# Token weights of the experts: spread by a product on TensorE, or by broadcast reads from DRAM

## What is computed

```python
x = x + cross_attention(layernorm(x), ctx, ctx, mask, Wq, Wk, Wv, Wo)   # 16 heads of 8
flat = layernorm(x)                                                     # 2048 tokens x 128
logits = flat @ router_w.T                                              # 16 experts
topk_scores, topk_idx = top_k(logits + router_bias, 2)
combine[token, topk_idx] += softmax(topk_scores)                        # 2048 x 16, two entries per token
hidden = silu(gate_all(flat)) * up_all(flat)                            # each expert: 64 hidden features
out = sum over experts of combine * (hidden @ down) + shared_expert(flat)   # shared: 128 hidden features
x = x + out
```

## Time and profile before

| | us |
|---|---|
| device time, median of 3 runs | 201.56 (201.18 to 201.57) |
| span of the profiled execution | 199.7 |
| TensorE busy | 184.6 (92%) |
| VectorE busy | 169.6 (85%) |
| ScalarE busy | 128.1 (64%) |
| GpSimd busy | 94.5 (47%) |

### The profile page before, as it was taken

One profiled execution on the slowest core, in us unless ns is written; L12 is line 12 of the kernel. 1 busy time (PEld: TensorE's weight loads), 2 busy tenths in 40 slices (PEclk: granted clock), 3 DMA queues, 4 the chain that ended last, 5 costly groups with the idle time before them and its releaser, 6 DMA issues.

```text
span 199.7 us, 4422 instructions
## 1 busy us (share of the span) xinstructions
PE 184.6 (92%) x1389; PEld 132.0 (66%) x1397; DVE 169.6 (85%) x520; ACT 128.1 (64%) x298; POOL 94.5 (47%) x156
## 2 busy tenths in 40 slices
PE   7497599999999999999995999999999999999973
PEld 7375456566666666676683677677777777777742
DVE  6899999799899999999998789867887798778881
ACT  2195448789999889989986555564554544555531
POOL 6855992968888888888785802400000000000000
PEclk9999999999999999999999699999999999999999
DMA  5978700000000000000000000000100010001001
GB/s 130 302 219 207 303 14 0 5 0 3 2 3 2 0 0 0 0 3 0 5 2 0 0 3 0 0 0 0 54 3 0 0 53 0 0 0 53 0 0 53
DMA packets 8095, 7.07 MB, mean 35 GB/s; under 512 B 784, under 2 KB 7056, under 8 KB 7952
## 3 DMA queue, kind: packets, MB, share of 16 engines
q1 hardware_dynamic: 7504, 6.34, 10.4%
q10 hardware_dynamic: 576, 0.55, 1.1%
HBM read 5.84 MB, written 1.05 MB: 34 GB/s over the span
## 4 chain that ended last, share of the span: by engine, by line
PE 78%; DVE 7%; issue 1%; ACT 1%; DVEq 0%; ACTq 0%
PE bank L1026 38%; PE bank L982 14%; PE bank L964 7%; PE bank L973 5%; PE bank L1066 3%; PE bank L953 2%; PE bank L943 2%; DVE xn L678 2%; PE bank L933 2%; PE bank L938 1%; PE bank L922 1%; PE bank L949 1%; DVE v_all L805 1%; PE bank L1031 1%; PE bank L1038 1%
## 5 line engine op out<-in xcount | busy, mean ns | idle before, releaser
L613 ACT ACTIVATE sig<-bank 128x512 f32<-128x512 f32 x36 | 21.4, 598 | 34.9 <-PE bank L1026 34.6
L982 PE MATMUL bank<-k_blk,q_blk 128*128 128x512 f32 x64 | 34.0, 615 | 0.2 <-issue 0.2
L827 DVE TENSOR_TENSOR hid_u<-sig,bank 128x512 f32<-128x512 f32 x32 | 22.0, 686 | 13.3 <-PE bank L1026 10.2
L442 POOL TENSOR_TENSOR k_blk<-k_all,consts_sb 128x512 f32<-128x512 f32 x32 | 32.7, 1042 | 0.0
L1026 PE MATMUL bank<-xt_hi,w_hi 128*128 (+1 forms) x72 | 30.0, 416 | 0.0
L1026 PE MATMUL bank<-xt_hi,w_lo 128*128 (+1 forms) x72 | 28.8, 400 | 0.0
L1026 PE MATMUL bank<-xt_lo,w_hi 128*128 (+1 forms) x72 | 28.8, 400 | 0.0
L764 DVE TENSOR_REDUCE smax<-bank 128x8 f32<-128x512 f32 x32 | 22.0, 686 | 1.8 <-PE bank L982 1.8
L568 ACT COPY prob_t<-bank 128x512 f32<-128x512 f32 x32 | 18.7, 585 | 7.0 <-PE bank L964 6.7
L785 DVE TENSOR_TENSOR prob<-bank,smax 128x512 f32<-128x512 f32 x32 | 22.0, 687 | 0.6
L1026 PE MATMUL bank<-hid_hi,w_hi 128*128 128x512 f32 (+1 forms) x37 | 20.5, 554 | 1.1 <-DVE hid_lo L836 1.1
(11 more groups left out here) (127 smaller groups left out, 399.0 us busy)
## 6 DMA issues: line engine op xcount, KB each, us to landing
w_moe_sb<-w_moe SPq DMA_DIRECT2D x1, 1728.0 KB, 8.1
x_sb<-x SPq DMA_DIRECT2D x4, 256.0 KB, 7.4
ctxt_sb<-ctx_t SPq DMA_DIRECT2D x4, 256.0 KB, 6.1
ctx_sb<-ctx_nat SPq DMA_DIRECT2D x4, 256.0 KB, 5.1
out<-x_sb SPq DMA_DIRECT2D x3, 256.0 KB, 2.3
w_att_sb<-w_att ACTq DMA_DIRECT2D x1, 264.0 KB, 5.8
mrow<-mask_row ACTq DMA_DIRECT2D x1, 256.0 KB, 5.4
sel_sb<-expert_sel SPq DMA_DIRECT2D x1, 256.0 KB, 8.3
```

Of the source, the lines that this page charges most:

```text
L442: last = nc.gpsimd.tensor_tensor(k_blk[p][:, g, :, :], k_all[:, bass.ds(t, 1), g, :].broadcast_to([P, HG, S]), hmask_sb.rearrange("p (h o) ...
L613: nc.scalar.activation(sig[r][:, :], gate_ps[r][:, :], ACT.Silu).then_inc(s_sig, 1)
L827: nc.vector.tensor_tensor(dst[:, :], sig[r][:, :], up_ps[r][:, :], ALU.mult).then_inc(s_hid_u, 1)
L982: nc.tensor.matmul(score_ps[g][:, :], q_blk[q][:, g, :, :].rearrange("p b s -> p (b s)"), k_blk[q][:, g, :, :].rearrange("p h s -> p (h s) ...
```

## The change

`sel_sb`, `identb_sb`, `comb3` and the product `token_weights` go. `weights_as_rows` turns `comb` of a half (8 tiles x 16 experts on 128 columns) by one f32 transpose into a part of bank 2; it waits for the sum and for an earlier copy out of that bank, and `attention_transposed(15)`, which writes the same bank, now waits until the transpose is copied. `weights_to_sbuf` copies 128x128 elements into `comb_t`, for the first half between `silu(0,1)` and step 16. SP stores this to `w_rows` in DRAM, waits until it has landed, and then issues for each unit two broadcast loads: the row of one expert, 512 tokens, over 64 partitions, twice. The target `spread` is a ring of four buffers (`SPREADS`, in the memory of `mix_all`); a later round waits for `weighted` four units earlier. SP's `store_result` now stands between these loads. `weighted` waits for both loads and reads `spread`. `up` no longer waits for the bank of the spread weights. VectorE's routing of the first half ends with the sum. `half_tiles`, `two_weights` and `join_experts` are the old lines in functions of their own.

```diff
+        spread = [mix_all[:, k * GT:(k + 1) * GT, :].rearrange("p t k -> p (t k)") for k in range(SPREADS)]
+        w_rows = nc.dram_tensor("w_rows", [2, EXPERTS, TILES // 2, P], F32).ap()
...
-        def expert_weights(eng, ops, half, written):
...
-            for part in range(PARTS - 1):
-                ops.tensor_copy(comb3[:, :, part, :], comb[:, tiles, :]).then_inc(written, 1)
-                eng.wait_ge(written, 3 + 2 * part)
-                ops.tensor_tensor(comb[:, tiles, :], comb[:, tiles, :], comb3[:, :, part, :],
-                                  ALU.subtract).then_inc(written, 1)
-                eng.wait_ge(written, 4 + 2 * part)
-            ops.tensor_copy(comb3[:, :, PARTS - 1, :], comb[:, tiles, :]).then_inc(s_comb3, 1)
+        def weigh_experts(ops, half):
+            tiles = half_tiles(half)
             for k, dst in ((0, comb), (1, comb_b)):
+                last = ops.tensor_tensor(dst[:, tiles, :], dst[:, tiles, :],
+                                         w_top[:, tiles, k:k + 1].broadcast_to([P, TILES // 2, EXPERTS]), ALU.mult)
+            last.then_inc(s_route[half], 1)
+        def join_experts(eng, ops, half):
+            tiles = half_tiles(half)
+            eng.wait_ge(s_route[half], 1)
+            ops.tensor_tensor(comb[:, tiles, :], comb[:, tiles, :], comb_b[:, tiles, :], ALU.add).then_inc(s_comb[half], 1)
...
-            sp.dma_start(sel_sb[:, :, :], expert_sel).then_inc(s_wmoe, 16)
-            sp.dma_start(identb_sb[:, :], ident_bf).then_inc(s_wmoe, 16)
+            def store_rows(half):
+                sp.wait_ge(s_ct_sb, half + 1)
+                sp.dma_start(w_rows[half].rearrange("e t k -> t e k"), comb_t[half][:, :]).then_inc(s_w_rows, 16)
+            def spread_weights(n):
+                g, pair = divmod(n, EPAIRS)
+                if n >= SPREADS:
+                    sp.wait_ge(s_hid, n - SPREADS + 1)
+                for e in range(2):
+                    rows = w_rows[g // 2, 2 * pair + e, (g % 2) * GT:(g % 2 + 1) * GT, :]
+                    sp.dma_start(spread[n % SPREADS][e * E_DIM:(e + 1) * E_DIM, :],
+                                 rows.rearrange("(o t) k -> o (t k)", o=1).broadcast_to([E_DIM, GN]))\
+                        .then_inc(s_spread[n % SPREADS], 16)
...
+            store_rows(0)
+            sp.wait_ge(s_w_rows, 16)
+            for n in range(GROUPS * EPAIRS):
+                if n == EPAIRS + SPREADS:
+                    store_rows(1)
+                    sp.wait_ge(s_w_rows, 32)
+                spread_weights(n)
+                if n >= EPAIRS and n % EPAIRS == SPREADS + 1:
+                    store_result(n // EPAIRS - 1)
+            for n in range(GROUPS - 1, GROUPS + 1):
+                store_result(n)
...
-            nc.gpsimd.memset(comb_t[:, :].bitcast(F32), 0.0).then_inc(s_comb_zero, 1)
...
+            def weights_to_sbuf(half):
+                act.wait_ge(s_ct, half + 1)
+                nc.scalar.copy(comb_t[half][:, :], ct_ps[half]).then_inc(s_ct_sb, 1)
...
             silu(0, 1)
+            weights_to_sbuf(0)
             peel(step, TILES)
-            weights_to_sbuf(0, cb_ps[0], slice(0, GN))
             high_part(0, 1)
-            weights_to_sbuf(1, cb_ps[0], slice(GN, 2 * GN))
...
             def weighted(g, m):
                 dve.wait_ge(s_hid_u, n + 1)
-                dve.wait_ge(s_cb, g * EPAIRS + m)
-                nc.vector.tensor_tensor(hid[m % 3][:, :], hid_u[r][:, :], cb_ps[r][:, :], ALU.mult).then_inc(s_hid, 1)
+                k, turns = (m - 1) % SPREADS, EPAIRS // SPREADS
+                dve.wait_ge(s_spread[k], (g * turns + (m - 1) // SPREADS + 1) * 32)
+                nc.vector.tensor_tensor(hid[m % 3][:, :], hid_u[r][:, :], spread[k], ALU.mult).then_inc(s_hid, 1)
...
+            def weights_as_rows(half):
+                pe.wait_ge(s_comb[half], 1)
+                pe.wait_ge(s_at_sb, TILES - 1 + half)
+                nc.tensor.transpose(ct_ps[half], comb[:, half_tiles(half), :].rearrange("p t e -> p (t e)"),
+                                    ident_sb).then_inc(s_ct, 1)
...
-            def token_weights(g, m):
-                pe.wait_ge(s_ct_sb, min(m, 2) if isinstance(g, int) else 4)
-                nc.tensor.matmul(cb_ps[m % 2][:, :], sel_sb[:, m - 1, :], comb_t[:, bass.ds(g * GN, GN)], start=True,
-                                 stop=True).then_inc(s_cb, 1)
...
             up(0, 1)
+            weights_as_rows(0)
+            pe.wait_ge(s_ct_sb, 1)
             attention_transposed(TILES - 1, 1)
-            weights_as_rows(0, cb_ps[0])
```

## The result

The changed kernel takes 196.66 us (median of 4 runs, 195.19 to 197.24) where the kernel before takes 201.56 (201.18 to 201.88): a ratio of 0.9743, 95% interval 0.9701 to 0.9786. The time lies in the range of the prediction (192.2 to 197.0), but above its forecast of 192.4 to 194.4, 3.3 us over the 193.4 that it named. The profiled execution is the slowest of the four (197.24, span 195.4), so the traces miss by a little more than the medians: 195.4 against the 191.5 us that the sum gave for the span.

A forecast was written before the change was run, and what follows sets the result against it. TensorE, never idle in the expert stage, was taken as the bound. Hand-over 1.4 + products 6.7 + transposes 0.4 - VectorE's other work 0.3 = 8.2 us, so 201.56 falls to 193.4 us (forecast 192.4 to 194.4, range 192.2 to 197.0).

The forecast's parts named there:

- Part 1: Expert stage on TensorE: 29 dropped spreading products of 0.23 us give 6.7 us, fewer second-half transposes 0.4 us.
- the 0.3 us charged for VectorE's other work in group 0: Group 0's five remaining slots: VectorE's top-two and second-half routing leave too little slack; 0.3 us lost, bounds 0 to 2.9.
- Part 2: Routed slot: VectorE and ScalarE loop low_part, weighted, high_part takes 2.04 us, below TensorE's 2.09, so TensorE stays the bound.
- Rival (c): Expert stage: the VectorE and ScalarE loop takes 2.2 us and becomes the bound, giving 196.6 us; chance 0.14.
- Part 3: Hand-over between stages: weighted(0,1) waits for DRAM until 111.8 us, gate(0,4) starts at 115.3 instead of 116.68; 1.4 us gained.
- the second trip: Hand-over: broadcast loads from DRAM before weighted(0,1), 0.4 us for the second issue plus 2.3 us landing, bounds 1.9 to 5.4.
- the signs that the prediction named: First weighted in the next profile: near 111.8 us confirms the hand-over forecast, after 113 us means a late first trip.
- rival (a): Hand-over: the first trip is late, weighted(0,1) at 113 to 115.5 us, time 194.6 to 197.1 us; chance 0.13.
- Rival (b): After TensorE's new hand-over wait: clock falls to half speed for 3.4 us, costing 1.7 us, giving 195.1 us; chance 0.17.
- Part 4: Later units' broadcasts: four buffers allow 8.4 us a round, at most 6.9 needed, so they stay hidden; nothing charged.
- Rival (d): Expert stage: broadcasts become the bound, slower than before from 2.61 us a unit, 213.6 us at 3.0; chance 0.05.
- the two conditions named for its lower end: Range's lower end: no cost from VectorE's other work in group 0, and both DRAM trips taking 1.9 us; 192.2 us.

The follow-up runs named there:

- e4: Changed kernel with one more unread 512-column product in each of 29 TensorE slots, in place of the dropped one; 200.95 us, ratio 0.9998 to the kernel before.
- e2: Changed kernel with ten unread products filling TensorE's gap before norm_transposed(15); 195.10 us, ratio 0.9698 to the kernel before.
- e3: Changed kernel whose first four group 0 units read wrong weights loaded early, so no transfer is waited for; 194.19 us, ratio 0.9659 to the kernel before.
- e5: Changed kernel with gate doing two of its three products; 196.2 us in a single execution.
- e1: Changed kernel run again, unedited; 197.49 us, ratio 0.9789 to the kernel before.
- e6: Changed kernel with the weights' transpose ahead of up(0,1) and its copy on VectorE instead of ScalarE; 194.76 us, ratio 0.9692 to the kernel before.
- e7: e6 plus seven unread products before norm_transposed(15); 195.13 us, ratio 0.9713 to the kernel before.
- e8: e6 plus five unread products, with ScalarE's queue issuing one of the first unit's two broadcasts; 194.20 us, ratio 0.9671 to the kernel before.
- e10: e6 with GpSimd's low parts of the expert weights regrouped 3, 3, 3, away from the first weighted; 195.31 us, ratio 0.9699 to the kernel before.
- e11: e8 with GpSimd's low parts regrouped 3, 1, 3, 2 over steps 14 to 17; 195.21 us, ratio 0.9689 to the kernel before.
- e9: e8 with GpSimd's low parts regrouped 3, 3, 3 over steps 14 to 16; 195.84 us, ratio 0.9727 to the kernel before.

## Why the prediction was right and where it was wrong

**Part 1, the products: right in groups 1 to 3, wrong in group 0.** Between the last `weighted` of group 0 and the last of all, before takes 63.95 us and after 57.60: 6.35 gained, where the sum had 24 x 0.23 + 0.4 = 5.9. e4 takes 5.06 of it back with 24 products. But the five products in `slot(0,4)` to `slot(0,8)` (5 x 0.23 = 1.15 us of the 6.7) gave nothing: from `weighted(0,3)` to `weighted(0,8)` before takes 11.60 us, and e2 and e4 both take 11.57. The term that failed is the 0.3 us charged for VectorE's other work in group 0, the last tile's top two and the second half's routing. Before, TensorE was the bound there, as the earlier trace rows say, and VectorE stood waiting for it at the turn to group 1:

```profile
130.75 0.69 DVE L827 TENSOR_TENSOR hid<-sig,bank 128x512 f32<-128x512 f32 x1 [1.19 <-PE bank L1026]
```

With shorter slots on TensorE that slack is gone. In e2 VectorE waits for no product of TensorE from `weighted(0,3)` to `weighted(0,8)`, and its own order fills the 11.57 us: five units at the loop's 2.05 us are 10.25, and 0.54, 0.52 and 0.25 us come on top, for step 18, for `top_two(1)` with a `low_part` of 0.90 us and for a `weighted` of 0.94 us (the last section has the reason of these two). The prediction saw the work and charged 0.3 us for it; it took all of the 1.15. The new wait is not the reason: e3, which does not wait, needs 11.56 us for the same way.

**Part 2, the loop: right.** A steady unit of the changed kernel, VectorE and ScalarE by time, the answer to the earlier trace rows:

```profile
143.34 0.69 DVE L838 TENSOR_TENSOR hid_lo<-hid,hid_hi 128x512 fp32r<-128x512 f32 x1 [0.16 <-ACT hid_hi L622]
...
143.95 0.68 DVE L846 TENSOR_TENSOR cmix_sb<-hid_u,mix_all 128x512 f32<-128x512 f32 x1
...
144.67 0.62 ACT L622 CAST hid_hi<-cmix_sb 128x512 fp32r<-128x512 f32 x1 [0.29 <-DVE cmix_sb L846]
...
145.40 0.69 DVE L838 TENSOR_TENSOR hid_lo<-cmix_sb,hid_hi 128x512 fp32r<-128x512 f32 x1 [0.16 <-ACT hid_hi L622]
```

0.61 + 0.72 + 0.73 = 2.06 us against the 2.04 forecast. e5 shows this loop as the floor. Rival (c), a loop of 2.2 us, did not come. That `weighted` costs the same from SBUF holds here, but not beside GpSimd (last section).

**Part 3, the hand-over: the path and the steps right, the second trip mis-sized.** With the 1.18 us of the late start taken off, the copy ends at 106.90 (forecast about 107.0) and `attention_transposed` starts at 106.95 (forecast 107.05). The store trip took 2.24 us from its issue to the next issue, forecast 2.1. The second trip is the term that failed: 0.4 + 2.3 = 2.7 us forecast, 3.63 measured (110.34 to 113.97), with an issue of 0.51 and a landing of 2.98. The value was taken from the 128 KB store and a small load, as if the queue's being empty decided. But two broadcasts ran at once, and later ones do no better. Transfers of the changed kernel, KB and median us from issue to landing:

```profile
mix_all<-w_rows SPq DMA_DIRECT2D x64, 128.0 KB, 2.9
```

So 2.9 us is what this pattern takes; no run times a broadcast by itself, so whether the pair or the pattern costs it stays open. By the signs that the prediction named, the first `weighted` is at 113.97 us just past the 113 of rival (a), and with the late start taken off, at 112.79, between the forecast and that rival.

**Rival (b), the clock, came in the profiled execution** and in e1 and e5, for 1.16 to 1.4 us up to `gate(0,4)`; it had been put at 1.7 with a chance of 0.17. The forecast took VectorE's wait for 1.4 us; it was 2.57, and TensorE's gap 2.58. Of the four profiled gaps over 2.5 us (after, e1, e4, e5) three were followed by a clock of 0.50; of six gaps of 0.27 to 1.51 us (e2, e6, e7, e8, e10, e11) none. In the kernel before, 2.05 us without a product, until 107.95 us, came ahead of the 0.50 of the earlier trace rows. The length alone doesn't decide it: e4's gap of 2.65 us was not followed by a drop. Why not, was not settled. So a part of e2's gain may be the luck of an execution, as in e4. The Trainium skill, "TensorE: Matmul & The Clock Gate", section "HAM oscillation — how this bites in real kernels", tells of matmul bursts that run slow after each transfer wait; three of these four gaps agree with it and one does not.

**Part 4, the later transfers: right.** Waits of VectorE for transfers in the whole execution, total us, times, longest:

```profile
DVE hid L846 <- DMA mix_all<-w_rows: 2.6, 1, 2.6
```

One wait, the first. Rival (d) needed all of them.

**The rest of the 3.9 us.** 1.18 us are the late start, and 1.05 of them the clock of 0.50 at 24 to 27 us (13.47 against 12.42 us under e1), before anything that the change touches on the path. Nothing in the trace of before could have shown it, since that execution had none. It comes and goes between executions of one kernel.

In sum: 1.18 (late start, most of it the clock) + 0.99 (trips) + 1.16 (clock behind the wait) + 0.57 (the last column) = 3.9 us. The 0.57 are, but for rounding, the five products that paid nothing where only 0.3 had been charged (0.85), and 0.13 by which after takes longer than before from `gate(0,4)` to `weighted(0,8)`, less the 0.45 that groups 1 to 3 gave beyond the forecast. So the time fell into the range because the range had room for rival (b), with chance against the forecast in the first column; the size of the gain was not foreseen. What e6 and e8 win in the hand-over they lose in part, for their last column is 0.4 us longer than e2's: in e6 to e11 the fourth and fifth `weighted` of group 1 stand 2.40 us apart, 2.05 in after and e2, and in e6 `hid_lo` waits 0.51 us there instead of 0.16. The reason was not pursued. One sum of the prediction is off without bearing on this: the two conditions named for its lower end give back 0.3 + 0.6 us, which makes 192.5 and not 192.2.

## What to carry to other kernels

When work leaves the bound engine, the gain counts only where that engine still sets the pace after the change: where another engine is then full, as VectorE is in group 0, the work removed beside it pays nothing. A trip through DRAM on the path is priced from a row of its own pattern, two broadcasts at once here, and shortened by starting it sooner (e6) rather than by another queue (e8). And before an idle engine's work is moved to make room, look at what the other engine reads there: the wait may only move, as in e9.

## What was not expected of the hardware

VectorE operations with both operands in SBUF were held by GpSimd operations on SBUF that had begun before them, until these ended: 1.48 and 1.50 us instead of 0.69 for `weighted` in e7 and e3, each ending 0.54 us after GpSimd's, and 0.69 again in e9 without it. The prediction read two rows of equal length and wrote "no change" for a `weighted` that reads SBUF in place of PSUM; those rows come from a stretch in which GpSimd does nothing. The kernel before has the sign of it in its hand-over. GpSimd and VectorE by time:

```profile
112.29 1.98 POOL L472 TENSOR_TENSOR w_lo<-w_moe_sb,w_hi 128x384 fp32r<-128x384 f32 x2
...
113.32 0.69 DVE L827 TENSOR_TENSOR hid_u<-sig,bank 128x512 f32<-128x512 f32 x1 [0.59 <-PE bank L1026]
113.92 0.90 DVE L836 TENSOR_TENSOR hid_lo<-hid,hid_hi 128x512 fp32r<-128x512 f32 x1
```

`hid_u`, with one operand in PSUM, takes its 0.69 us beside GpSimd; `hid_lo`, with two in SBUF, takes 0.90 and ends 0.55 us after GpSimd's pair. The Trainium skill, "SBUF — State Buffer", section "Who interferes with whom", states this rule: a VectorE instruction with two SBUF inputs and a GpSimd instruction that reads SBUF share a read port, and whichever came first keeps the other out to its end. The runs agree, the other way round too: in e6, where `weighted` begins ahead of the second of GpSimd's two operations, the pair takes 2.42 us (111.16 to 113.58) instead of 1.96. The change took `weighted` from the one kind to the other; in the profiled execution of after the first one escaped, since GpSimd's pair ended as the transfer landed (112.03 + 1.96 = 113.99 us). The sixth `weighted` of group 0 did not, in after as in every changed kernel. GpSimd's sum of the second half and VectorE in after:

```profile
126.22 0.79 POOL L340 TENSOR_TENSOR comb<-comb,comb_b 128x128 f32<-128x128 f32 x1
126.61 0.94 DVE L846 TENSOR_TENSOR hid<-hid_u,mix_all 128x512 f32<-128x512 f32 x1
```

It ends at 127.55 us, 0.54 us after GpSimd's; in the kernel before the same unit took 0.68 us with one operand in PSUM. The `low_part` ahead of it (125.79 + 0.90) ends 0.54 us after GpSimd's product of the weights (125.74 + 0.41).
